# Loads laid out per group, the last two groups in halves, and a new order for every engine

## The chip, the cores and the metric

The kernel runs on one core of one Trainium2 chip. The metric is the device time of one execution in microseconds (us). A core has five engines that run in parallel, each taking its own instructions strictly in order: TensorE (PE in the profile, its weight loads PEld), VectorE (DVE), ScalarE (ACT), GpSimd (POOL) and SyncE (SP), which here only issues DMA transfers. They wait for one another by semaphores.

## The reference

Two graph layers run on 64 graphs of 128 nodes with 128 features. `adj` holds 0 or 1 in these inputs, so of the four kinds of edge in the attention layer and of the 40 relations in the second only the first occurs:

```python
e = leaky_relu(einsum('bid,bjd->bij', x * a_0, x), 0.2)     # attention scores
alpha = softmax(where(adj == 1, e, -9e15))                    # over j
y = layernorm(x + alpha @ x)
h = y @ W_loop.T
v = (h + b_loop) * sigmoid(h @ Wg_loop.T + bg_loop)
out = layernorm(y + relu((adj == 1).T @ v))
```

Values other than 0 and 1 in `adj` are answered by a slow general path at the end, which is entered only when a sum over `adj` says so. It is not entered here.

## The kernel before

The 64 graphs are 16 groups of four. Everything is done by group, in float32, as a chain of stages; a stage is one call in the code, named `stage:group` here. `products` (PE, L988) multiplies the weighed, transposed x into the scores of four graphs and adds a penalty where there is no edge (L991, from the tile `absent`). `relu` and `scores` make the leaky scores and their row maximum (DVE L877), `exp` the probabilities (ACT L775), `turn_probs` transposes them on PE (L1007), `turned_probs` copies that out of PSUM, `attend` multiplies them with x (PE L1017, tile `p_o`), `residual1` divides and adds x (DVE L883 and L888), `stats1` takes mean and variance (DVE L896), `norm1` makes the inverse root on POOL (L667 to L676), and `y_v`, `y_s`, `y_p` write the normalized y on DVE, ACT and POOL, by the table `Y_BY`. `turn_y` (PE L1033) and `turned_y` transpose y, `gates` is the product with both weight matrices (PE L1045, tile `p_hg`), `tanhs` the gate on ACT (L822), `values` gate times value on DVE (L917), `sums` the sum over neighbours (PE L1062), `residual2`, `stats2` (DVE L929, L952) and `norm2` (POOL L696 to L712) the second normalization. The table `OUT_BY` says who writes the output: POOL alone for groups 0 to 9 (L705 and L718, inside `norm2`), DVE and ACT (`finish_v`, `finish_s`) for groups 10 to 15. `store` sends it out.

Each of the five engines takes its stages in the order of one list by hand, `ORDER`. Nothing reorders them later, so an engine whose next stage has to wait keeps all that stands behind it waiting. Most tiles have two buffers, group g taking number g % 2; the PSUM tiles `p_o`, `p_e`, `p_ut`, `p_yt`, `p_hg` and `p_ag` have one.

`load_scores:g` fetches the transposed x (`x_t`) and `adj` of a group, `load_values:g` x itself; each is 256 KB on SP's queue, as 512 runs of 512 bytes (only `adj` of group 0 goes through ACT's queue). `load_weights` fetches the matrices of all three directions, two of which only the general path reads; `prepare_w`, `mix_weights` and `evac_weights` turn the loop direction's into `w_both`. The last group alone has its `sums`, `residual2`, `stats2` and `store` in halves of two graphs: their sums go to `p_ut` and `p_e`, which are free by then.

Of the kernel before, what the change touches and what calls it, by code (L numbers as in the profile page):

```python
# [33 lines left out]
OUT_BY = ["pppp"] * 10 + ["vvss"] * 5 + ["vvvs"]  # L34
# [19 lines left out]
        weigh_s:11 exp:10 tanhs:5 weigh_s:12 relu_s:11 y_s:7 exp:11 turned_y:6 mask:6 y_s:8 turned_probs_s:10
        relu_s:12 weigh_s:13 tanhs:6 exp:12 turned_y:7 weigh_s:14 y_s:9 turned_probs_s:11 relu_s:13 weigh_s:15 tanhs:7
        absent:14 turned_probs_s:12 turned_y:8 exp:13 mask:8 relu_s:14 y_s:10 tanhs:8 turned_y:9 exp:14 y_s:11 tanhs:9
        turned_probs_s:13 relu_s:15 turned_y:10 mask:10 exp:15 tanhs:10 turned_probs_s:14 turned_y:11 y_s:12
        turned_probs_s:15 tanhs:11 turned_y:12 y_s:13 tanhs:12 mask:12 turned_y:13 finish_s:10 y_s:14 tanhs:13
# [1045 lines left out]
```

## Time and profile before

| | |
|---|---|
| median of 3 runs | 114.0 us (113.84 to 115.27) |
| the profiled execution's own time | 113.89 us |
| span of its profile | 112.10 us |
| busy: PE, DVE, ACT, POOL | 99.2, 95.5, 88.5, 80.9 us |
| granted TensorE clock | 0.977 of full speed over the span, full speed until 106 us |

The span runs from the first to the last event of the core; 1.79 us of the execution's own time lie around it. Busy is the time in which at least one instruction of the engine was under way. A matmul record of the 128x128 kind lasts about 0.27 us, though the next follows after 0.11 us, so a busy PE is not a PE without gaps.

### The profile page before, as it was taken

The page shows a single profiled execution, that of the slowest core. Times are in us where ns is not written, and L with a number is a line of the kernel's source. Part 1 is how long each engine was busy: PE and PEld are TensorE (multiplying, and loading weights), DVE is VectorE, ACT ScalarE, POOL GpSimd, SP SyncE. Part 2 cuts the span into 40 slices and gives each one's busy share as a digit, 9 for nine tenths or more (in the row PEclk, how much of TensorE's full clock was granted, in tenths as well). Part 3 has the DMA queues.
Part 4 walks back from the last instruction along what each step waited for, and adds up shares of the span by engine and source line. Part 5 has one row for each costly group of instructions (what it writes and reads, how often), then busy time and mean ns, then how long its engine had stood idle before and what let it go on. Part 6 is the DMA issues. An engine that isn't in the chain of part 4 may idle for free.

```text
span 112.1 us, 2748 instructions
## 1 busy us (share of the span) xinstructions
PE 99.2 (89%) x684; PEld 88.7 (79%) x684; DVE 95.5 (85%) x376; ACT 88.5 (79%) x220; POOL 80.9 (72%) x158
## 2 busy tenths in 40 slices
PE   6997879999999999999999999999999998999000
PEld 6964767989999999998999899988899794979000
DVE  0178899799899999999998999998997999788850
ACT  4168659989999999999899989949977885896140
POOL 5004792358826799989899999999998988855560
PEclk9999999999999999999999999999999999999955
DMA  0999999999999604990423025527212030333324
GB/s 10 306 290 291 290 315 308 293 287 283 285 293 292 174 3 121 266 260 13 128 63 94 0 79 145 159 76 204 66 50 79 3 96 0 94 94 88 105 64 126
DMA packets 34771, 17.36 MB, mean 155 GB/s; under 512 B 1218, under 2 KB 34755, under 8 KB 34755
## 3 DMA queue, kind: packets, MB, share of 16 engines
q1 hardware_dynamic: 34082, 16.91, 56.6%
q10 hardware_dynamic: 672, 0.26, 0.9%
q8 instruction: 6, 0.10, 0.4%
q14 instruction: 11, 0.08, 0.2%
HBM read 12.98 MB, written 4.19 MB: 153 GB/s over the span
## 4 chain that ended last, share of the span: by engine, by line
POOL 35%; PE 27%; issue 14%; DVE 10%; ACT 5%; DMA 5%; POOLq 1%; SPq 0%; ACTq 0%; DVEq 0%
POOL rs L708 8%; POOL cent L705 7%; POOL rs L672 7%; PE p_hg L1045 6%; PE p_o L1017 5%; DMA inputs<-x_t 5%; PE p_ag L1062 3%; PE p_e L988 3%; POOL out_s L718 3%; PE p_ut L1007 3%; POOL y L687 2%; PE p_yt L1033 2%; POOL rs L696 2%; DVE res L888 2%; POOL minus L669 2%
## 5 line engine op out<-in xcount | busy, mean ns | idle before, releaser
L1045 PE MATMUL p_hg<-w_both,y_t 128*128 128x256 f32 x128 | 30.8, 384 | 0.5 <-ACT y_t L814 0.3
L1045 PEld LDWEIGHTS p_hg<-w_both,y_t 128*128 128x128 f32 x128 | 23.2, 190 | 3.8 <-ACT y_t L814 1.0
L775 ACT ACTIVATE prob<-nscore,nmax 128x128 f32<-128x128 f32 x64 | 20.3, 396 | 2.7 <-DVE nmax L877 2.6
L888 DVE SCALAR_TENSOR_TENSOR res<-p_o,rz,inputs 128x128 f32<-128x128 f32 x64 | 18.0, 344 | 1.4 <-POOL y L687 0.9
L1017 PE MATMUL p_o<-inputs,prob_t 128*128 128x129 f32 x128 | 17.2, 276 | 0.8 <-DVE prob_t L866 0.8
L1017 PEld LDWEIGHTS p_o<-inputs,prob_t 128*128 128x128 f32 x128 | 15.7, 191 | 1.7 <-DVE prob_t L866 1.0
L672 POOL TENSOR_TENSOR rs<-rs,minus_half 128x4 f32<-128x4 f32 x16 | 16.7, 1042 | 0.0
L708 POOL TENSOR_TENSOR rs<-rs,minus_half 128x4 f32<-128x4 f32 x16 | 16.3, 1020 | 0.0
L1062 PE MATMUL p_ag<-vals,mask 128*128 128x128 f32 x120 | 16.0, 276 | 0.3 <-DVE vals L917 0.3
L1062 PEld LDWEIGHTS p_ag<-vals,mask 128*128 128x128 f32 x120 | 14.9, 191 | 0.8 <-issue 0.6
L988 PE MATMUL p_e<-inputs,xat 128*128 128x128 f32 x104 | 13.9, 277 | 0.0
L656 POOL TENSOR_TENSOR xat<-inputs,a_col 128x512 f32<-128x512 f32 x6 | 6.2, 1041 | 10.6 <-DMA inputs<-x_t 7.9
L792 ACT ACTIVATE y<-res,shift,rs 128x128 f32<-128x128 f32 x26 | 11.7, 488 | 2.2 <-POOL shift L676 2.2
L822 ACT ACTIVATE th<-p_hg 128x256 f32<-128x256 f32 x32 | 11.3, 379 | 2.6 <-PE p_hg L1045 2.5
L988 PEld LDWEIGHTS p_e<-inputs,xat 128*128 128x128 f32 x104 | 12.9, 192 | 0.5 <-DVE nmax L877 0.2
L917 DVE SCALAR_TENSOR_TENSOR vals<-th,p_hg 128x256 f32<-128x256 f32 x32 | 12.1, 413 | 1.1 <-ACT th L822 1.0
L877 DVE CUSTOM_DVE_ANT_0 nscore<-p_e,rel 128x128 f32<-128x128 f32 x52 | 11.9, 285 | 0.7 <-ACT rel L767 0.7
L952 DVE BATCH_NORM_STATS2 st<-res 128x6 f32<-128x256 f32 x32 | 12.1, 420 | 0.1
L896 DVE BATCH_NORM_STATS2 st<-res 128x6 f32<-128x256 f32 x32 | 12.1, 419 | 0.0
L929 DVE SCALAR_TENSOR_TENSOR res<-p_ag,y 128x512 f32<-128x512 f32 x15 | 10.3, 684 | 1.4 <-POOL out_s L718 0.7
L1033 PE MATMUL p_yt<-ident,y 128*128 128x128 f32 x64 | 10.8, 278 | 0.5 <-ACT y L792 0.2
L718 POOL TENSOR_TENSOR out_s<-cent,rs 128x512 f32<-128x512 f32 x10 | 10.4, 1041 | 0.8
(88 smaller groups left out, 177.1 us busy)
## 6 DMA issues: line engine op xcount, KB each, us to landing
inputs<-x_t SPq DMA_DIRECT2D x16, 256.0 KB, 5.2
inputs<-x SPq DMA_DIRECT2D x16, 256.0 KB, 5.3
inputs<-adj SPq DMA_DIRECT2D x15, 256.0 KB, 5.3
out<-out_s SPq DMA_DIRECT2D x15, 256.0 KB, 2.4
inputs<-adj ACTq DMA_DIRECT2D x1, 256.0 KB, 4.5
out<-out_s SPq DMA_DIRECT2D x2, 128.0 KB, 1.9
w_rows<-w SPq DMA_DIRECT2D x1, 192.0 KB, 4.9
wg_s<-wg_t SPq DMA_DIRECT2D x1, 192.0 KB, 4.7
```

The lines of the kernel that those rows point to most:

```text
L672: nc.gpsimd.tensor_tensor(rs1[:, k, 1], rs1[:, k, 0], minus_half[:], ALU.pow).then_inc(rstd1_done, 1)
L708: nc.gpsimd.tensor_tensor(rs2[:, k, 1], rs2[:, k, 0], minus_half[:], ALU.pow).then_inc(rstd2_done, 1)
L718: nc.gpsimd.tensor_tensor(out_s[:, k], cent[:], rs2[:, k, 1, :, None].broadcast_to([P, G, P]), ALU.mult).then_inc(out_by_p, 1)
L775: nc.scalar.activation(prob[:, k, i], nscore[:, k, i], ACT.Exp, scale=-1.0, bias=nmax[:, k, i:i + 1]).then_inc(exp_done, 1)
L888: nc.vector.scalar_tensor_tensor(out=res1[:, k, i], in0=p_o[:, i // 2, i % 2, 0:P], scalar=rz[:, k, i:i + 1], in1=x_s(g)[:, i, 0:P], op0=A ...
L896: nc.vector.bn_stats(st1[:, k, half(h)].rearrange("p a c -> p (a c)"), res1[:, k, half(h)].rearrange("p a d -> p d a")).then_inc(st1_done, 1)
L917: nc.vector.scalar_tensor_tensor(out=vals[:, k, half(h)], in0=th[:, k, half(h)], scalar=1.0, in1=p_hg[:, half(h), 0], op0=ALU.add, op1=ALU ...
L988: nc.tensor.matmul(e_bank(g)[:, i], xat[:, k, i], xt(g)[:, i], start=(i == 0), stop=False, skip_group_check=True)
L1017: last = nc.tensor.matmul(p_o[:, i // 2, i % 2, 0:P + 1], prob_t[:, g % 2, i], x_s(g)[:, i], start=True, stop=True)
L1033: last = nc.tensor.transpose(p_yt[:, i], y[:, g % 4, i], ident[:])
L1045: last = nc.tensor.matmul(p_hg[:, i], y_t[:, g % 2, i], w_both[:], start=True, stop=True)
L1062: last = nc.tensor.matmul(p_sum[:, i], mask[:, s * G + i], vals[:, g % 2, i], start=True, stop=True)
```

## The change

- `x_t` and `adj` are laid out on the host so that the four graphs of a group lie side by side in a row: a group's transfer is 128 runs of 2 KB in place of 512 runs of 512 bytes. x and the output keep their runs of 512 bytes.
- `load_weights` fetches the loop direction alone; `load_others` fetches the other two later, under a semaphore of its own.
- The last two groups (`SPLIT`) run in halves from the gates on: gates, tanhs, values, sums, residual2, stats2, norm2, finish and store. The sums of group 14 go to `p_ag` and `p_o`, those of group 15 to `p_ut` and `p_e`. Their outputs are written by DVE alone (before: two graphs of group 14 and one of group 15 by ACT).
- All five lists of `ORDER` are new.

```diff
-OUT_BY = ["pppp"] * 10 + ["vvss"] * 5 + ["vvvs"]
+OUT_BY = ["pppp"] * 10 + ["vvss"] * 4 + ["vvvv"] * 2
...
     "gpsimd": """
-        ... norm2:9
-        norm2:10 norm1:14 norm1:15 norm2:11 norm2:12 norm2:13 norm2:14 norm2:15
+        ... norm2:8 norm1:14
+        norm2:9 norm2:10 norm2:11 norm1:15 norm2:12 norm2:13 norm2_h0:14 norm2_h1:14 norm2_h0:15 norm2_h1:15
...
-        load_scores:0 load_scores:1 load_values:0 load_scores:2 load_scores:3 load_scores:4 load_scores:5
-        load_values:1 load_weights:0 load_values:2 load_scores:6 load_scores:7 load_values:3 load_values:4
+        load_scores:0 load_scores:1 load_scores:2 load_scores:3 load_weights:0 load_scores:4 load_values:0
+        load_scores:5 load_scores:6 load_values:1 load_scores:7 load_values:2 load_values:3 load_values:4
...
-        last_ag = (p_ut, p_e)
+        late_ag = ((p_ag[:, 0:2], p_o[:, 0, :, 0:P]), (p_ut[:, 0:2], p_e[:, 0:2]))
...
-                sp.dma_start(xt(g), x_t_v[g]).then_inc(xt_loaded[g], 16)
+                sp.dma_start(xt(g).rearrange("p g d -> p (g d)"), x_t[g]).then_inc(xt_loaded[g], 16)
...
+            def load_others(g):
+                sp.dma_start(w_rows[:, FWD:], w[FWD:].rearrange("k f d -> f k d")).then_inc(others_loaded, 16)
+                sp.dma_start(wg_s[:, FWD:], wg_t[FWD:].rearrange("k f e -> f k e")).then_inc(others_loaded, 16)
...
+            def norm2_half(g, h):
+                k = g % 2
+                moved = [i for i in graphs_by("s", OUT_BY, g) if i // 2 == h]
+                pool.wait_ge(st2_done, 2 * g + h + 1)
+                all_out(pool, g - 2)
+                nc.gpsimd.tensor_scalar(rs2[:, k, 0, half(h)], st2[:, k, half(h), 2], 1.0 / P, EPS, ALU.mult, ALU.add)\
+                    .then_inc(var2_done, 1)
+                pool.wait_ge(var2_done, normed(g, h))
+                nc.gpsimd.tensor_tensor(rs2[:, k, 1, half(h)], rs2[:, k, 0, half(h)], minus_half[:, half(h)], ALU.pow)\
+                    .then_inc(rstd2_done, 1)
...
-            def gates(g):
+            def gates(g, hs=(0, 1)):
...
-                for h in range(2):
+                for h in hs:
                     if g >= 1:
                         pe.wait_ge(vals_done[h], g)
...
+    def rows_of_groups(a):
+        a = np.asarray(a)
+        return a.reshape(a.shape[0] // G, G, P, P).swapaxes(1, 2).reshape(a.shape[0] // G, P, W)
```

Three places of the new order follow, each as the built kernels have it. In the changed kernel norm1 stands on L702 to L711 and norm2 on L731 to L753 (its halves on L761 and L764); PE's products are L1054 and L1057, turn_probs L1073, attend L1083, turn_y L1099, gates L1111 and sums L1132.

POOL near the end, before: norm1:15 (L667 to L676), then norm2:11 (L696 to L712).

```order
L667 TENSOR_SCALAR rs<-st 128x4
L669 TENSOR_SCALAR minus<-st 128x3
L672 TENSOR_TENSOR rs<-rs,minus_half 128x4
L676 TENSOR_TENSOR shift<-minus,rs 128x3
L696 TENSOR_SCALAR rs<-st 128x4
L700 TENSOR_SCALAR minus<-st 128x2
L708 TENSOR_TENSOR rs<-rs,minus_half 128x4
L712 TENSOR_TENSOR shift<-minus,rs 128x2
```

POOL at the same place, now: norm2:11 (L731 to L747), then norm1:15.

```order
L731 TENSOR_SCALAR rs<-st 128x4
L735 TENSOR_SCALAR minus<-st 128x2
L743 TENSOR_TENSOR rs<-rs,minus_half 128x4
L747 TENSOR_TENSOR shift<-minus,rs 128x2
L702 TENSOR_SCALAR rs<-st 128x4
L704 TENSOR_SCALAR minus<-st 128x3
L707 TENSOR_TENSOR rs<-rs,minus_half 128x4
L711 TENSOR_TENSOR shift<-minus,rs 128x3
```

The last group's norm1 has changed places with norm2:11, which has to wait for stats2:11.

PE's last stages, before: gates:14, turn_y:15, sums:13, gates:15, sums:14, and sums:15 in halves.

```order
L1045 MATMUL p_hg<-w_both,y_t 128x256 x4
L1033 MATMUL p_yt<-ident,y 128x128 x4
L1062 MATMUL p_ag<-vals,mask 128x128 x4
L1045 MATMUL p_hg<-w_both,y_t 128x256 x4
L1062 MATMUL p_ag<-vals,mask 128x128 x4
L1062 MATMUL p_ut<-vals,mask 128x128 x2
L1062 MATMUL p_e<-vals,mask 128x128 x2
```

PE's last stages, now: the first half of gates:14, sums:13, the other half, turn_y:15, half of sums:14, gates:15, and three more halves of sums.

```order
L1111 MATMUL p_hg<-w_both,y_t 128x256 x2
L1132 MATMUL p_ag<-vals,mask 128x128 x4
L1111 MATMUL p_hg<-w_both,y_t 128x256 x2
L1099 MATMUL p_yt<-ident,y 128x128 x4
L1132 MATMUL p_ag<-vals,mask 128x128 x2
L1111 MATMUL p_hg<-w_both,y_t 128x256 x4
L1132 MATMUL p_o<-vals,mask 128x128 x2
L1132 MATMUL p_ut<-vals,mask 128x128 x2
L1132 MATMUL p_e<-vals,mask 128x128 x2
```

sums:13 has moved ahead of turn_y:15, and less work stands behind turn_y:15.

PE's first stages after products:0, before: products:1, turn_probs:0, attend:0, products:2, turn_probs:1, products:3.

```order
L988 MATMUL p_ag<-inputs,xat 128x128 x4
L991 MATMUL p_ag<-absent,penalties 128x512
L1007 MATMUL p_ut<-ident,prob 128x128 x4
L1017 MATMUL p_o<-inputs,prob_t 128x129 x4
L988 MATMUL p_yt<-inputs,xat 128x128 x4
L991 MATMUL p_yt<-absent,penalties 128x512
L1007 MATMUL p_ut<-ident,prob 128x128 x4
L988 MATMUL p_hg<-inputs,xat 128x128 x4
L991 MATMUL p_hg<-absent,penalties 128x512
```

The same place, now: products:1, turn_probs:0, products:2, products:3, turn_probs:1, attend:0.

```order
L1054 MATMUL p_ag<-inputs,xat 128x128 x4
L1057 MATMUL p_ag<-absent,penalties 128x512
L1073 MATMUL p_ut<-ident,prob 128x128 x4
L1054 MATMUL p_yt<-inputs,xat 128x128 x4
L1057 MATMUL p_yt<-absent,penalties 128x512
L1054 MATMUL p_hg<-inputs,xat 128x128 x4
L1057 MATMUL p_hg<-absent,penalties 128x512
L1073 MATMUL p_ut<-ident,prob 128x128 x4
L1083 MATMUL p_o<-inputs,prob_t 128x129 x4
```

The first attend has moved behind two products and a turn_probs, as x of group 0 has moved back in SP's list. ACT's list now has absent:2 and mask:0 ahead of exp:1.

## Rows read from the trace of the kernel before

**Rows 1.** The page: span, busy time by engine, and GB/s in 40 slices.
```profile
span 112.1 us, 2748 instructions
PE 99.2 (89%) x684; PEld 88.7 (79%) x684; DVE 95.5 (85%) x376; ACT 88.5 (79%) x220; POOL 80.9 (72%) x158
...
GB/s 10 306 290 291 290 315 308 293 287 283 285 293 292 174 3 121 266 260 13 128 63 94 0 79 145 159 76 204 66 50 79 3 96 0 94 94 88 105 64 126
```

**Rows 2.** The table of two windows, columns in its first line.
```profile
core 0: us, PE busy (x) PEld busy (x) DVE busy (x) ACT busy (x) POOL busy (x), PEclk, DMA share, GB/s
39.20:94.10 54.90, 54.19 (x382) 49.22 (x381) 52.01 (x197) 47.86 (x119) 51.07 (x85) 1.00 0.35 97
22.00:38.00 16.00, 16.00 (x119) 14.93 (x118) 14.93 (x67) 15.51 (x38) 10.27 (x24) 1.00 1.09 286
```

**Rows 3.** Timeline of POOL: start, us, instruction, idle time before it.
```profile
39.22 0.20 POOL L696 TENSOR_SCALAR rs<-st 128x4 f32<-128x4 f32 x1
...
42.47 0.20 POOL L696 TENSOR_SCALAR rs<-st 128x4 f32<-128x4 f32 x1
...
53.53 0.59 POOL L687 TENSOR_SCALAR y<-res,minus,rs 128x128 f32<-128x128 f32 x1
...
90.22 0.20 POOL L696 TENSOR_SCALAR rs<-st 128x4 f32<-128x4 f32 x1
...
92.08 0.20 POOL L667 TENSOR_SCALAR rs<-st 128x4 f32<-128x4 f32 x1
...
94.12 0.20 POOL L667 TENSOR_SCALAR rs<-st 128x4 f32<-128x4 f32 x1
...
95.95 0.20 POOL L676 TENSOR_TENSOR shift<-minus,rs 128x3 f32<-128x3 f32 x1
```

**Rows 4.** Timeline of the first 17 us: what waited for the loads, and exp:1.
```profile
9.17 1.04 POOL L656 TENSOR_TENSOR xat<-inputs,a_col 128x512 f32<-128x512 f32 x1 [7.15 <-DMA inputs<-x_t]
...
10.59 1.28 ACT L775 ACTIVATE prob<-nscore,nmax 128x128 f32<-128x128 f32 x4 [0.31 <-DVE nmax L877]
...
10.94 1.04 POOL L656 TENSOR_TENSOR xat<-inputs,a_col 128x512 f32<-128x512 f32 x1 [0.73 <-DMA inputs<-x_t]
...
11.79 1.06 ACT L740 ACTIVATE absent<-inputs 128x1024 bf16<-128x1024 int32 x1
...
15.39 1.06 ACT L740 ACTIVATE absent<-inputs 128x1024 bf16<-128x1024 int32 x1 [2.44 <-issue]
```

**Rows 5.** Timeline of DVE: the stages of one group, from scores:5 on.
```profile
22.54 0.29 DVE L877 CUSTOM_DVE_ANT_0 nscore<-p_e,rel 128x128 f32<-128x128 f32 x1 [0.67 <-ACT rel L767]
...
23.39 0.18 DVE L883 RECIPROCAL rz<-p_o 128x4 f32<-128x4 f32 x1
...
24.64 0.75 DVE L896 BATCH_NORM_STATS2 st<-res 128x6 f32<-128x256 f32 x2
...
25.31 0.60 DVE L907 SCALAR_TENSOR_TENSOR y<-res,st,rs 128x128 f32<-128x128 f32 x2
...
25.83 0.74 DVE L917 SCALAR_TENSOR_TENSOR vals<-th,p_hg 128x256 f32<-128x256 f32 x2
...
29.77 0.69 DVE L929 SCALAR_TENSOR_TENSOR res<-p_ag,y 128x512 f32<-128x512 f32 x1
```

**Rows 6.** Timeline of the last 14 us: PE, POOL, DVE and SP.
```profile
98.24 0.60 PE L1033 MATMUL p_yt<-ident,y 128*128 128x128 f32 x4
...
99.99 1.99 PE L1045 MATMUL p_hg<-w_both,y_t 128*128 128x256 f32 x8 [0.26 <-ACT y_t L814]
...
103.16 0.61 PE L1062 MATMUL p_e<-vals,mask 128*128 128x128 f32 x4
...
106.82 0.20 POOL L696 TENSOR_SCALAR rs<-st 128x4 f32<-128x4 f32 x1
...
108.36 0.90 DVE L944 SCALAR_TENSOR_TENSOR out_s<-res,st,rs 128x128 f32<-128x128 f32 x3 [1.20 <-POOL rs L708]
...
109.70 0.47 SPq L630 DMA_DIRECT2D out<-out_s  x1
```

More of the change, by code:

```diff
@@ L54 @@
[L54 to L58, printed above, removed]
@@ L76 @@
+        residual2:11 stats2:11 stats1:15 finish_v:10 values:13 residual2:12 finish_v:11 stats2:12 y_v:15 values_h0:14
+        residual2:13 stats2:13 values_h1:14 finish_v:12 residual2_h0:14 finish_v:13 stats2_h0:14 values_h0:15
+        residual2_h1:14 values_h1:15 stats2_h1:14 residual2_h0:15 stats2_h0:15 residual2_h1:15 stats2_h1:15
+        finish_v_h0:14 finish_v_h1:14 finish_v_h0:15 finish_v_h1:15
         """,
     "gpsimd": """
[L78 removed]
@@ L534, in groups_of @@
             by = stage[-1]
+            if stage[-3:] in ("_h0", "_h1"):
+                by = stage[-4]
+                if stage.startswith("finish_"):
+                    return [g for g in SPLIT if by in OUT_BY[g][half(int(stage[-1]))]]
+                return SPLIT
+            if stage in ("gates", "tanhs", "values", "sums", "residual2", "stats2", "norm2", "store"):
+                return [g for g in range(n_groups) if g not in SPLIT]
             if stage in PAIRED:
                 return PAIRED[stage]
-            if stage in ("load_weights", "prepare_w", "mix_weights", "evac_weights"):
+            if stage in ("load_weights", "load_others", "prepare_w", "mix_weights", "evac_weights"):
                 return [0]
@@ L547, in groups_of @@
             if stage.startswith("finish_"):
-                return [g for g in range(n_groups) if by in OUT_BY[g]]
+                return [g for g in range(n_groups) if g not in SPLIT and by in OUT_BY[g]]
             return range(n_groups)
@@ L576, in out_groups, with normed, shifts, out_made_half @@
             return sum(by in of for of in OUT_BY[:max(0, g + 1)])
+        def normed(g, h=1):
+            before = g + sum(of < g for of in SPLIT)
+            return before + (h + 1 if g in SPLIT else 1)
+        def shifts(g, h=1):
+            before = out_groups("s", g - 1) + sum("s" in OUT_BY[of][0:2] and "s" in OUT_BY[of][2:4]
+                                                  for of in SPLIT if of < g)
+            if g not in SPLIT:
+                return before + 1
+            return before + sum("s" in OUT_BY[g][half(i)] for i in range(h + 1))
+        def out_made_half(by, g, h):
+            return out_made(by, g - 1) + OUT_BY[g][:2 * h + 2].count(by)
         def graphs_by(by, table, g):
```

206 lines of the change are left out of this document (120 added, 86 removed).

## The prediction

> **What bounds the kernel now.** I read the page first [rows 1]: PE is busy for 99.2 of 112.1 us and DVE for 95.5, ACT 88.5, POOL 80.9, so nobody is a bound with room to spare and the shares alone decide nothing. Then the windows [rows 2]. From 39.2 to 94.1 us PE is busy for 54.19 of 54.90 us, DVE for 52.01, and POOL, which the page had last, for 51.07; from 22 to 38 us POOL has only 10.27 of 16 while PE has all 16 and DVE 14.93. Then POOL's own timeline [rows 3]. At 39.22 norm2:0 starts, at 94.12 norm1:15, and the pieces in between fill the stretch (the 3.8 us that are not busy are short gaps between instructions that need each other, and lie inside the pieces). A norm2 that also writes the output takes 42.47 - 39.22 = 3.25 us, a norm1 94.12 - 92.08 = 2.04, the y of one graph about 0.55, a norm2 without output 92.08 - 90.22 = 1.86. Ten, nine, five and one of these are 32.5 + 18.4 + 2.75 + 1.86 = 55.5 us, where 54.9 were measured. So POOL runs without a pause from 39.2 us until the last y can be made (its shift at 95.95), and it is what lets group 15 into the second layer. PE and DVE follow close behind it. The end hangs on a chain [rows 6]: turn_y:15 at 98.24, gates:15 at 99.99, the last sums at 103.16 to 103.77, POOL's last norm2 at 106.82 (POOL had norm2:14 before it), the last three outputs on DVE from 108.36 to 109.26, the last store issued at 109.70 and the end of the span at 112.1. From the last sum to the end that is 8.33 us.
>
> **The sum is made against the profiled execution**, 112.1 us of span and 113.89 us of its own time, 1.79 us around it. That execution lies 0.1 us under the median of 114.0. A measurement of this kernel can tell about 2%, 2.3 us, from no change.
>
> **The head: the new layout.** In the trace of before, x_t:2, the sixth transfer, lands at 9.17, x_t:3, the eighth, at 10.94, and adj:5, the thirteenth, at 15.39, where ACT had waited for it [rows 4]. That is 6.22 us for seven, 0.889 us for 256 KB, and counted back 3.84 us before the first. Nothing in the trace has runs of 2 KB. The bounds are 0.889 (no gain), and the fastest slice of the load phase, 315 GB/s [rows 1], 0.83 us; I take 0.83 and keep 0.889. A gain beyond 315 GB/s isn't excluded; its worth is small, as the next steps show. New order: adj:3 is the eighth, not the ninth, and lands at 3.84 + 8 x 0.83 = 10.5 (at 0.889: 11.0; before 11.8). absent:2 takes 1.06 us and its read-out, mask:0 as much, and only then comes exp:1 with 1.28: it ends at 10.5 + 1.2 + 1.1 + 1.3 = 14.1, where before it ended at 11.87. So turn_probs:1, the DVE copy of it (a 512-wide pass, 0.69 us as in [rows 5]) and attend:0 end at 14.2, 15.0 and 16.0. x of group 0, now at position 11.5, lands at 13.4 (14.1 at 0.889) and is in time.
>
> From there DVE sets the pace, with the prices of [rows 5]: four scores 0.85, residual1 1.25 (I use 1.3), stats 0.7, y 0.6, values 0.74, residual2 0.69. From attend:0 at 16.0: residual1:0 to 17.3, stats1:0 18.0, turned_probs:2 18.7, scores:4 19.6, residual1:1 20.9, stats1:1 21.6, y:0 22.2, scores:5 23.0, residual1:2 24.3, stats1:2 25.1. Before it ended at 25.39 with the same stages done. x of group 1 (position 16.5: 17.5, or 18.5) is needed by attend:1 for residual1:1 at 19.6, so it is in time at either pace. **The head is worth -0.3 us** with 0.83, +0.2 with 0.889. The weights of the other directions, 256 KB that go behind the early loads, are in this count. load_others is free: only the general path waits for it, and behind it on SP stand the loads of groups 10 and later.
>
> A rule of the Trainium skill speaks against the layout (DMA: Bandwidth & Descriptors, Specifications): transfers reach line rate from 512 bytes up. The runs of before have just that, so by this rule the pace stays 0.889 and the sum is 0.5 us higher. The same page (Why small descriptors are slow) gives a fixed cost of about 3 cycles for each packet beside one cycle for 32 bytes; an estimate from it is 4 x 19 cycles against 67, a pace of 0.78, and the sum would be some 0.3 us lower. No run here shows either yet.
>
> **The middle: norm2 earlier.** DVE's list now has residual2:0 and stats2:0 right behind scores:7. From 25.1 the stages ahead are y, scores, residual1, values, stats, y, residual1, stats, y, scores, residual2, stats: 9.8 us, and 0.7 more for the 7% that DVE idles here [rows 2], so norm2:0 starts at 35.6 and ends at 38.9; before it started at 39.22, and POOL idled 5.7 us between 22 and 38. norm1:5, done by 39.2 before, comes behind it at 39.0 (stats1:5 is 3.4 us of DVE further on). What POOL then has until the end of norm1:15: nine norm2 (29.3), eleven norm1 (22.4), six y (3.3) and two short norm2 (3.7), 58.7 us, less the 0.6 by which the same sum was too long before: 58.1. So norm1:15 ends at **97.1, 1.0 us later than before**, though norm2:11 now stands ahead of it with 1.86 us: the earlier start pays only half of it. The last y is then written by ACT (three passes, about 1.3 us) and turn_y:15 can't end before 98.8; by PE's work it stands 0.9 us (sums:13) further back than before. Between 98.24 and 98.24 + 0.9 = 99.1 I put its start at 98.5.
>
> **The tail: halves.** Behind turn_y:15 there were sums:13, gates:15, sums:14, sums:15, now only half of sums:14, gates:15 and three halves of 0.45 us. turn_y:15 ends at 98.9, tanh and the copy by ACT follow to 99.6, gates:15 runs 99.7 to 101.4, and the last half of the sums, which waits for a tanh behind finish_s:13, ends at 103.0, against 103.77. On DVE stats of the first half of group 14 end at 101.4, behind finish_v:13. POOL has four half norm2: from 106.82 to 108.36 it took 1.54 us for a whole one with a small extra instruction of 0.2 [rows 6], so 1.3 us each if half the width costs the same. The nearest row of less work is the small multiplication of 0.20 us [rows 3], which bounds the power from below; I take the full price, since the row is the same operation. They end at 102.8, 104.6, 105.9 and 107.2 (the second waits for its stats at 103.2). DVE adds the 0.9 us of three graphs that ACT wrote before, but in the shadow of POOL, and its last half (two graphs, 0.6 us) ends at 107.9. At the low end POOL is never waited for: DVE's stats of the last half end at 104.7, and four halves of the output of 0.6 us each end at 107.1 to 107.2. The last store no longer stands behind another (0.4 us): issued at 107.9, and 2.4 us to the end as before (109.70 to 112.1) gives 110.3, or 109.6.
>
> **The sum:** span between 109.6 and 110.3, and I take 110.0: 2.1 us less. With 1.79 around it the time is **111.8 us**, 1.9% under the median. If the cover goes (POOL late), the halves cost up to two powers more, 2 us, and the tail gives nothing.
>
> **Rivals.**
> - *The runs of 2 KB are no faster.* By the pace of [rows 4] everything in the head stands 0.5 us later: 112.3 us. For it: 290 GB/s in nearly every slice may be a limit of the memory and not of the runs.
> - *The new order opens holes elsewhere.* In 54.9 us of the middle PE has 0.7 us idle, DVE 2.9, POOL nothing but its short gaps [rows 2, 3]. An order so tight has little to win and can lose: two holes of 0.7 us on POOL, or norm2:0 no earlier than before, and the result is 113.3 us. Against it: POOL had 5.7 us of idle to give.
> - *POOL is ahead by more.* If DVE doesn't idle on its way to stats2:0 and the power on two elements is short, norm1:15 ends at 96.2 and the tail follows PE, -1.5 us: 110.3 us.
> - *Slower: norm2:11 in front of norm1:15.* On POOL norm2:11 must wait for stats2:11, which hangs on sums:11, behind attend:15 and gates:12 on PE. POOL comes to it at 97.1 - 2.04 - 1.86 = 93.2 us. Each us by which stats2:11 ends later moves norm1:15, the last y and the end by one us. From 95.3 us on the kernel is slower than before; at 96.4 it is 115.0 us. For it: before, residual2:11 was on DVE only at 92.8. Against it: its place on DVE is now ahead of stats1:15.
>
> **How the numbers follow.** Forecast 0.32 (its own range 110.9 to 112.7), no faster runs 0.18, holes 0.18, POOL ahead 0.22, norm2:11 late 0.10. Faster by over 2% means under 111.7: all of POOL ahead, a good 0.4 of the forecast, a third of the case of no faster runs, together 0.42. Slower by over 2%, above 116.3, is the far part of the last case, 0.04, and 0.54 are left. The range reaches from the case of POOL ahead with a margin, 109.6, to the upper side of the holes, 114.3; outside lie some 0.15, most of it the case of norm2:11.
>
> **What would show it.** Right: GB/s of the load phase above 315; the first norm2 of POOL at 35 to 37 us; no idle on POOL from there until norm1:15 ends at about 97; half norm2 of 1.3 us; the last sum at 103 and the end 7.3 us behind it. Wrong: a wait of POOL for stats2:11 or stats1:15 near 93, a wait of PE for y before turn_y:15, DVE idle above 3 us in the middle, or attend:0 waiting for x.

## The result, and the profile after

| kernel | median us | lowest to highest | runs | span of the profiled execution |
|---|---|---|---|---|
| before | 114.12 | 113.84 to 115.27 | 4 | 112.1 |
| after | 109.38 | 109.15 to 109.69 | 4 | 107.4 |

The ratio is 0.956, with a 95% interval of 0.951 to 0.961: 4.4% faster; by the medians it is 4.7 us. Six executions, four of layout_alone and two of after_norm1_first, ran at a lower granted clock and over 1.5% longer, and are left out of every ratio and median here. The forecast was 111.8 us with a range of 109.6 to 114.3, so the direction is right and the time lies 0.2 us below the range. The span was forecast at 110.0 and is 107.4.

The page of after, its first lines and the row of GB/s in 40 slices; they answer to [rows 1]:

```profile
span 107.4 us, 2765 instructions
PE 97.9 (91%) x677; PEld 89.4 (83%) x684; DVE 94.4 (88%) x380; ACT 87.1 (81%) x217; POOL 81.0 (75%) x158
...
GB/s 15 307 407 367 373 350 297 352 350 388 330 53 0 5 294 95 195 0 201 278 312 97 98 9 113 180 72 26 73 27 6 98 6 98 98 98 46 156 77 124
```

POOL has no less to do: it was busy for 80.9 us and is busy for 81.0, so on POOL the 4.7 us are idle time that is gone. DVE was busy for 95.5 us and PE for 99.2, now 94.4 and 97.9. The load phase runs at 350 to 407 GB/s in most slices where it ran at about 290.

The table of windows of after, columns in its first line, which answers to [rows 2]; the first two are of the load phase:

```profile
core 0: us, PE busy (x) PEld busy (x) DVE busy (x) ACT busy (x) POOL busy (x), PEclk, DMA share, GB/s
6.00:10.00 4.00, 3.55 (x24) 2.67 (x24) 3.21 (x16) 2.86 (x9) 2.08 (x2) 1.00 1.05 391
10.00:16.00 6.00, 5.95 (x43) 4.82 (x43) 5.86 (x31) 5.03 (x14) 3.12 (x3) 1.00 1.08 360
22.00:38.00 16.00, 15.95 (x117) 14.88 (x117) 15.42 (x68) 15.74 (x40) 12.55 (x26) 1.00 0.57 184
33.10:92.70 59.60, 58.70 (x429) 55.64 (x431) 56.74 (x221) 55.41 (x138) 54.49 (x95) 1.00 0.35 103
```

Between 22 and 38 us POOL does 12.55 us of work, where it did 10.27. That is the work it would otherwise have had to do at the end.

POOL's timeline of after (start, us, instruction, idle time before it), which answers to [rows 3]; L731 begins a norm2, L702 a norm1:

```profile
33.11 0.23 POOL L731 TENSOR_SCALAR rs<-st 128x4 f32<-128x4 f32 x1 [0.17 <-DVE st L1013]
...
36.72 0.20 POOL L702 TENSOR_SCALAR rs<-st 128x4 f32<-128x4 f32 x1 [0.18 <-DVE st L955]
...
38.95 0.20 POOL L731 TENSOR_SCALAR rs<-st 128x4 f32<-128x4 f32 x1 [0.40 <-DVE st L1013]
...
90.75 0.20 POOL L731 TENSOR_SCALAR rs<-st 128x4 f32<-128x4 f32 x1
...
92.66 0.20 POOL L702 TENSOR_SCALAR rs<-st 128x4 f32<-128x4 f32 x1
...
94.50 0.30 POOL L711 TENSOR_TENSOR shift<-minus,rs 128x3 f32<-128x3 f32 x1
```

norm2:0 starts at 33.11, 6.1 us earlier than before. After 38.95 POOL waits for no other engine until norm1:15 (one gap of 0.25 us, at 78, is its own), which starts at 92.66 although norm2:11 (90.75) now stands ahead of it, where it started at 94.12 without.

The head of after, timeline of POOL, ACT, PE and DVE; the first two rows answer to [rows 4], the last is stats1:2:

```profile
7.37 1.04 POOL L691 TENSOR_TENSOR xat<-inputs,a_col 128x512 f32<-128x512 f32 x1 [5.34 <-DMA inputs<-x_t]
...
9.36 1.04 ACT L795 ACTIVATE absent<-inputs 128x1024 bf16<-128x1024 int32 x1
...
12.93 1.07 PE L1083 MATMUL p_o<-inputs,prob_t 128*128 128x129 f32 x8
13.78 0.68 DVE L925 COPY prob_t<-p_ut 128x512 f32<-128x512 f32 x1
...
15.21 0.18 DVE L942 RECIPROCAL rz<-p_o 128x4 f32<-128x4 f32 x1
...
23.11 0.76 DVE L955 BATCH_NORM_STATS2 st<-res 128x6 f32<-128x256 f32 x2
```

x_t:2 is used at 7.37 instead of 9.17, absent:2 runs at 9.36 instead of 11.79, and stats1:2 ends at 23.87 instead of 25.39.

The tail of after, timeline of PE, POOL, DVE and SP, which answers to [rows 6]:

```profile
95.33 1.14 PE L1099 MATMUL p_yt<-ident,y 128*128 128x128 f32 x4
...
97.16 1.99 PE L1111 MATMUL p_hg<-w_both,y_t 128*128 128x256 f32 x8 [0.23 <-ACT y_t L871]
...
100.64 0.68 PE L1132 MATMUL p_e<-vals,mask 128*128 128x128 f32 x4 [0.23 <-DVE vals L976]
...
101.87 0.19 POOL L761 TENSOR_SCALAR rs<-st 128x2 f32<-128x2 f32 x1
102.15 0.69 POOL L764 TENSOR_TENSOR rs<-rs,minus_half 128x2 f32<-128x2 f32 x1
102.82 0.19 POOL L761 TENSOR_SCALAR rs<-st 128x2 f32<-128x2 f32 x1
103.10 0.70 POOL L764 TENSOR_TENSOR rs<-rs,minus_half 128x2 f32<-128x2 f32 x1
...
102.33 2.17 DVE L1005 SCALAR_TENSOR_TENSOR out_s<-res,st,rs 128x128 f32<-128x128 f32 x8
...
102.95 2.24 SPq L663 DMA_DIRECT2D out<-out_s  x4
```

turn_y:15 ends at 96.47, the last sums at 101.32, and from there to the end of the span it is 6.1 us, where it was 8.33. DVE writes all eight graphs in one piece of 2.17 us and waits for no power of POOL (the last one ends at 103.80, and the last two graphs, which need it, are a quarter of the piece).

### The profile page after: what moved, and what is told of

It is laid out like the page before. It is cut to its first block, busy times and chain, and to the rows that moved or that the text cites. A ratio compares the mean times of both kernels' runs of the same rounds, so it can differ in the third digit from the quotient of the medians.

```text
span 107.4 us, 2765 instructions
## 1 busy us (share of the span) xinstructions
PE 97.9 (91%) x677; PEld 89.4 (83%) x684; DVE 94.4 (88%) x380; ACT 87.1 (81%) x217; POOL 81.0 (75%) x158
## 4 chain that ended last, share of the span: by engine, by line
POOL 38%; DVE 23%; issue 18%; PE 14%; ACT 3%; POOLq 1%; DVEq 0%; ACTq 0%
POOL rs L707 9%; POOL cent L740 8%; POOL rs L743 7%; DVE nscore L936 5%; DVE res L947 5%; PE p_ag L1038 4%; PE p_hg L1111 3%; DVE rel L918 2%; POOL minus L704 2%; POOL out_s L753 2%; POOL rs L731 2%; PE p_e L1054 2%; POOL rs L702 2%; DVE out_s L1005 2%; POOL y L722 2%
## 5 line engine op out<-in xcount | busy, mean ns | idle before, releaser
L1111 PE MATMUL p_hg<-w_both,y_t 128*128 128x256 f32 x128 | 30.6, 381 | 0.9 <-ACT y_t L871 0.9
L1111 PEld LDWEIGHTS p_hg<-w_both,y_t 128*128 128x128 f32 x128 | 23.0, 190 | 3.8 <-ACT y_t L871 1.3
L1083 PE MATMUL p_o<-inputs,prob_t 128*128 128x129 f32 x128 | 17.2, 276 | 0.2 <-DVE res L947 0.2
L1083 PEld LDWEIGHTS p_o<-inputs,prob_t 128*128 128x128 f32 x128 | 15.9, 191 | 1.0 <-issue 0.7
L707 POOL TENSOR_TENSOR rs<-rs,minus_half 128x4 f32<-128x4 f32 x16 | 16.6, 1037 | 0.0
L1132 PE MATMUL p_ag<-vals,mask 128*128 128x128 f32 x116 | 15.4, 275 | 0.2
L1132 PEld LDWEIGHTS p_ag<-vals,mask 128*128 128x128 f32 x116 | 14.8, 191 | 0.4
L1054 PE MATMUL p_e<-inputs,xat 128*128 128x128 f32 x104 | 14.2, 281 | 0.2 <-DVE nmax L936 0.2
L743 POOL TENSOR_TENSOR rs<-rs,minus_half 128x4 f32<-128x4 f32 x14 | 14.3, 1021 | 0.0
L1054 PEld LDWEIGHTS p_e<-inputs,xat 128*128 128x128 f32 x104 | 13.3, 197 | 0.6 <-DVE nmax L936 0.4
L1073 PE MATMUL p_ut<-ident,prob 128*128 128x128 f32 x64 | 10.8, 280 | 0.5 <-ACT prob L830 0.4
L753 POOL TENSOR_TENSOR out_s<-cent,rs 128x512 f32<-128x512 f32 x10 | 10.4, 1041 | 0.8
L740 POOL TENSOR_TENSOR cent<-res,st 128x512 f32<-128x512 f32 x10 | 10.6, 1058 | 0.0
```

The source lines that it names most:

```text
L707: nc.gpsimd.tensor_tensor(rs1[:, k, 1], rs1[:, k, 0], minus_half[:], ALU.pow).then_inc(rstd1_done, 1)
L740: nc.gpsimd.tensor_tensor(cent[:], res2[:, k], st2[:, k, :, 1:2].broadcast_to([P, G, P]), ALU.subtract).then_inc(cent_done, 1)
L743: nc.gpsimd.tensor_tensor(rs2[:, k, 1], rs2[:, k, 0], minus_half[:], ALU.pow).then_inc(rstd2_done, 1)
L753: nc.gpsimd.tensor_tensor(out_s[:, k], cent[:], rs2[:, k, 1, :, None].broadcast_to([P, G, P]), ALU.mult).then_inc(out_by_p, 1)
L1054: nc.tensor.matmul(e_bank(g)[:, i], xat[:, k, i], xt(g)[:, i], start=(i == 0), stop=False, skip_group_check=True)
L1083: last = nc.tensor.matmul(p_o[:, i // 2, i % 2, 0:P + 1], prob_t[:, g % 2, i], x_s(g)[:, i], start=True, stop=True)
```

## The experiments

Each row has the kernel's ratio to the kernel before (measured beside it, with medians from 113.85 to 114.13) with its 95% interval, its median, and from its trace the starts of norm2:0 and norm1:15 on POOL, of turn_y:15 and of the last half of the sums on PE, and the end of the span, all in us.

| kernel | ratio | median | norm2:0 | norm1:15 | turn_y:15 | last sums | end |
|---|---|---|---|---|---|---|---|
| before | 1 | 114.0 | 39.22 | 94.12 | 98.24 | 103.16 | 112.1 |
| layout_alone | 1.006 (1.001 to 1.012) | 114.56 | 39.44 | 94.29 | 98.40 | 103.31 | 112.3 |
| before_halves | 0.999 (0.995 to 1.002) | 113.86 | 39.27 | 94.16 | 100.21 | 105.03 | 111.7 |
| before_halves_2 | 0.995 (0.991 to 0.999) | 113.48 | 39.12 | 93.95 | 98.07 | 103.26 | 111.2 |
| before_pool_load | 1.018 (1.017 to 1.020) | 115.98 | 39.21 | 96.11 | 100.22 | 105.15 | 114.1 |
| order_alone | 0.989 (0.984 to 0.994) | 112.79 | 34.47 | 93.83 | 96.51 | 101.50 | 110.9 |
| after_old_layout | 0.966 (0.958 to 0.974) | 110.41 | 34.41 | 93.77 | 96.45 | 101.75 | 108.6 |
| after_whole_groups | 0.978 (0.969 to 0.986) | 111.75 | 33.34 | 92.91 | 95.58 | 100.58 | 109.9 |
| after | 0.956 (0.951 to 0.961) | 109.38 | 33.11 | 92.66 | 95.33 | 100.64 | 107.4 |
| after_norm2_late | 0.985 (0.982 to 0.988) | 112.02 | 39.18 | 95.70 | 98.38 | 103.68 | 110.4 |
| after_pool_load | 0.979 (0.973 to 0.985) | 111.78 | 33.20 | 94.91 | 97.55 | 102.88 | 109.5 |
| after_dve_load | 0.976 (0.974 to 0.978) | 111.11 | 32.95 | 94.46 | 97.14 | 102.44 | 109.2 |
| after_norm1_first | 0.967 (0.961 to 0.973) | 110.34 | 33.00 | 90.96 | 96.15 | 101.62 | 108.5 |
| after_group9_by_act | 0.975 (0.972 to 0.978) | 111.07 | 32.77 | 94.15 | 96.59 | 102.09 | 108.9 |

### The layout, alone and taken back

layout_alone is the kernel before with the runs of 2 KB and nothing else:

```diff
-                sp.dma_start(xt(g), x_t_v[g]).then_inc(xt_loaded[g], 16)
+                sp.dma_start(xt(g).rearrange("p g d -> p (g d)"), x_t[g]).then_inc(xt_loaded[g], 16)
...
-                    sp.dma_start(adj_s(g), adj_v[g]).then_inc(adj_loaded[g], 16)
+                    sp.dma_start(adj_s(g).rearrange("p g d -> p (g d)"), adj_rows[g]).then_inc(adj_loaded[g], 16)
```

> The kernel before, with x_t and adj in runs of 2 KB and nothing else changed. The loads move at 367 to 407 GB/s in the trace after, against 290 before. Theory (the gain of the head is loads that land earlier, in an order that uses it): with the old order DVE is held at x_t:1, absent:2 and adj:5 only, some 1.0 to 1.5 us of its idle time before 17 us go, and since POOL is then bound from norm2:0 on, the end moves by about 1 us: 112.5 to 113.3. Rival A (the layout is the main part of the change): 111 or less. Rival B (the old order can't use it): 113.8 to 114.2.

Measured: 0.6% slower, and the end of the span at 112.3, so the theory's gain did not come. The transfers are about as fast as in after. The windows of layout_alone over the load phase:

```profile
6.00:10.00 4.00, 3.00 (x17) 1.77 (x15) 3.04 (x12) 3.18 (x9) 1.41 (x2) 1.00 1.06 379
10.00:16.00 6.00, 5.06 (x41) 4.78 (x42) 5.55 (x27) 4.64 (x13) 3.76 (x7) 1.00 1.11 361
```

absent:4 runs at 12.99 instead of 15.39, and still norm2:0 starts 0.2 us later. The timeline of layout_alone, POOL and DVE, shows where a loss can come from; the last row is residual1:1:

```profile
16.97 1.04 POOL L654 TENSOR_TENSOR xat<-inputs,a_col 128x512 f32<-128x512 f32 x1
...
17.16 1.26 DVE L905 SCALAR_TENSOR_TENSOR y<-res,st,rs 128x128 f32<-128x128 f32 x2
...
20.73 1.13 DVE L886 SCALAR_TENSOR_TENSOR res<-p_o,rz,inputs 128x128 f32<-128x128 f32 x4
```

In before the same two DVE passes take 0.61 us, from 17.13, and POOL runs nothing between 17.13 and 19.11, since its x_t comes later. Here POOL's pass over 512 columns is on at that time, DVE's passes take 0.65 us more, and residual1:1 starts 0.67 us later than in before (20.06). At this place the old order hangs on DVE's list and not on the transfers. That these 0.67 us are the whole of the loss at the end is not shown. The Trainium skill (SBUF — State Buffer, Who interferes with whom) says that a DVE instruction with two inputs in SBUF contends with a GpSimd instruction that reads SBUF, and calls the ports that they share an exclusive lock. If DVE's passes could start only behind POOL's, they would end at 18.01 + 0.60 = 18.6; the trace has 18.42, so it agrees with the contention, and the passes are not kept out for quite the whole of it.

after_old_layout is the same edit the other way: the kernel after with runs of 512 bytes for x_t and adj.

> The changed kernel with x_t and adj back in runs of 512 bytes; order, halves and late weights kept. Theory: the new order packs the loads close to use, so adj:3 and x of group 0 land 1 to 1.5 us later, attend:0 and all of the head follow, norm2:0 starts about 1.3 us later and POOL carries that to the end: 110.4 to 111.2. Rival A (layout is the main part): 112 or more. Rival B (the head has room): 109.3 to 109.7.

Measured: 1.0 us slower than after by the medians, 1.2 in the span. norm2:0 comes 1.3 us later, norm1:15 1.1, turn_y:15 1.1, the last sums 1.1. In the new order a later load passes through every stage to the end, in the old order it passes through none. Of the 6.1 us by which norm2:0 is earlier in after, the layout has 1.3 and the order 4.8.

### The order alone, the halves alone

order_alone has the new lists and the late weights, whole groups at the end, the outputs and the layout of before:

```diff
-OUT_BY = ["pppp"] * 10 + ["vvss"] * 4 + ["vvvv"] * 2
+OUT_BY = ["pppp"] * 10 + ["vvss"] * 5 + ["vvvs"]
...
-        ... gates_h0:14 sums:13 gates_h1:14 turn_y:15 sums_h0:14 gates_h0:15 gates_h1:15 sums_h1:14 sums_h0:15 sums_h1:15
+        ... gates:14 sums:13 turn_y:15 gates:15 sums:14 sums:15
...
-        ... norm2:13 norm2_h0:14 norm2_h1:14 norm2_h0:15 norm2_h1:15
+        ... norm2:13 norm2:14 norm2:15
```

> The new order with whole groups at the end, runs of 512 bytes; of the change only the order (with the late weights that are part of SP's list). The layout cost 1.0 us when it was taken from the changed kernel and the halves 2.4 us, so if the parts add up beside the order: 109.4 + 1.0 + 2.4 = 112.8 us (112.3 to 113.2). Rival (what bounds the end without the halves isn't the head, so the layout is hidden there): 111.7 to 112.0.

after_whole_groups is the same with the runs of 2 KB.

> The changed kernel with the end of before: groups 14 and 15 whole (only the last sums, residual and store in halves as before), two outputs of group 14 and one of group 15 by ACT again, the rest of the order as changed. Theory: the last sum comes at about 101.5 as in the changed kernel, and from there it takes 8.3 us as before instead of 6.1: 111.0 to 111.8. Rival (the halves only move work, the gain is all from norm2 and the loads being earlier): 109.2 to 110.2.

Measured against before: the order brings 1.1%, with the layout 2.2%, with the halves too 4.4%. By the medians the three steps are 1.2, 1.0 and 2.4 us. Steps taken one upon the other always add up to the whole; what tests the sum is order_alone, which was put at 112.8 us from the parts taken out of after one at a time, and took 112.79. So beside the new order the layout is worth 1.0 us with the halves and without them. What whole groups cost at the end is in the timeline of after_whole_groups, POOL and DVE:

```profile
102.41 0.20 POOL L703 TENSOR_SCALAR rs<-st 128x4 f32<-128x4 f32 x1 [1.75 <-DVE st L959]
...
104.25 0.20 POOL L703 TENSOR_SCALAR rs<-st 128x4 f32<-128x4 f32 x1
...
105.78 0.90 DVE L951 SCALAR_TENSOR_TENSOR out_s<-res,st,rs 128x128 f32<-128x128 f32 x3 [1.19 <-POOL rs L715]
```

The last sums start at 100.58, as in after (100.64). But POOL can begin norm2:14 only when all of group 14 has its stats (a wait of 1.75 us), norm2:15 has to stand behind it, and DVE waits 1.19 us for the last power. So the halves don't bring the sums forward; all of their 2.4 us lies behind the last sum.

before_halves and before_halves_2 put the halves on the kernel before, with its layout and its order up to group 13. They differ in the lists of the last two groups. The last stages of PE and ACT in the one and the other:

```diff
-PE:  gates_h0:14 sums:13 gates_h1:14 turn_y:15 sums_h0:14 gates_h0:15 gates_h1:15 sums_h1:14 sums_h0:15 sums_h1:15
+PE:  gates_h0:14 gates_h1:14 turn_y:15 sums:13 gates_h0:15 sums_h0:14 gates_h1:15 sums_h1:14 sums_h0:15 sums_h1:15
-ACT: tanhs:13 mask:14 turned_y:14 finish_s:11 tanhs_h0:14 y_s:15 tanhs_h1:14 turned_y:15 finish_s:12 tanhs_h0:15 ...
+ACT: mask:14 y_s:14 tanhs:13 turned_y:14 y_s:15 finish_s:11 tanhs_h0:14 tanhs_h1:14 turned_y:15 finish_s:12 tanhs_h0:15 ...
```

> The kernel before (its layout, its order until the last two groups, weights loaded early) with the halves at the end and its last two groups' outputs on DVE alone. Theory: the tail alone, 1.5 to 2.2 us less: 111.9 to 112.7. Rival (without the earlier POOL the halves find nothing to overlap, because turn_y:15 waits as before): 113.4 to 114.2.

> The kernel before with halves at the end, in a second list of the last two groups: the mask of groups 14 and 15 is made before y:14 and y:15 is written by ACT before the tanh of group 14, both of which stood in the way in the run before_halves (PE waited 0.83 us for the transposed y of group 14). Theory (in the old order the tail can gain only what POOL's late norm1:15 leaves; turn_y:15 starts at 98.2 as before, and from there half of the sums, the gates and three halves follow): last sum at 103.8 as before, end 6.1 us behind it: 111.6 to 112.6. Rival (the halves are worth nothing without the new order): 113.5 to 114.2.

The first gave nothing, because its list put the last mask ahead of the copy that PE waited for (0.83 us) and sums:13 (0.9) ahead of turn_y:15. The timeline of before_halves, ACT and PE:

```profile
95.81 1.05 ACT L812 ACTIVATE mask<-inputs 128x1024 f32<-128x1024 int32 x1
...
97.48 1.13 PE L1116 MATMUL p_hg<-w_both,y_t 128*128 128x256 f32 x4 [0.83 <-ACT y_t L876]
```

The end behind the last sum was short there too (6.7 us from its start, against 8.9 in before), but the sum itself started 1.9 us later. With the better list the sums are where they were, and 0.5 us is gained by the ratio (0.9 in the span of the profiled execution, the fastest of twelve), not 2.4. The median of 113.48 misses the theory and stands at the edge of the rival. The timeline of before_halves_2, POOL and DVE:

```profile
101.27 0.22 POOL L736 TENSOR_SCALAR rs<-st 128x4 f32<-128x4 f32 x1 [1.20 <-DVE st L1018]
...
105.34 0.41 DVE L998 SCALAR_TENSOR_TENSOR res<-p_e,y 128x256 f32<-128x256 f32 x1
```

From the last values at 102.69 on DVE waits for nobody, but behind them stands work that after has done ahead of them: the second residual2 of group 14 and two outputs of group 13 (0.60 us, at 103.69). So its last residual2 starts at 105.34, 2.1 us behind the last sum, where in after it is 0.9. Group 13 is late here from its sums on: sums:13 starts at 98.50 (93.58 in after), POOL waits 1.20 us for stats2:13, and norm2:13 starts at 101.27 (96.75 in after). Which part of the new order brings it forward, no run separates.

### Is POOL the bound, before and after?

after_pool_load and before_pool_load add two passes of 1.04 us, whose result nobody reads, to POOL ahead of norm2:3. The values of the kernel don't change.

```diff
             def norm2(g):
                 k = g % 2
+                if g == 3:
+                    for i in range(2):
+                        nc.gpsimd.tensor_tensor(extra[:, i], xt(0).rearrange("p g d -> p (g d)"),
+                                                a_col[:].broadcast_to([P, W]), ALU.mult).then_inc(extra_done, 1)
```

> The changed kernel with two more instructions on POOL, products of 128x512 into a tile that nobody reads, ahead of norm2:3 (1.04 us each, 2.1 us in all). Theory (POOL is saturated from norm2:0 to norm1:15 and carries the delay to the end): 1.7 to 2.2 us more, 111.1 to 111.6. Rival (PE and DVE are just as close and POOL has slack): under 1 us more, 109.5 to 110.3.

> The kernel before with the same two instructions of 1.04 us on POOL ahead of norm2:3. Theory (POOL is saturated from 39.2 us on here too): 1.7 to 2.3 us more, 115.7 to 116.4. Rival (before, the end hangs on PE or on the tail's own chain): under 1 us more.

Measured: the 2.08 us come out at the end whole in both. In before norm1:15 starts 1.99 us later and the end is 2.0 later; in after it is 2.25 and 2.1 (2.4 by the medians, slightly above the theory). So POOL had no slack from norm2:3 on in either order, as the sum of its pieces said ahead of the result.

after_norm2_late undoes the early norm2 alone:

```diff
-        y_p:4 norm2:0 norm1:5 norm2:1 y_p:5 norm1:6
+        y_p:4 norm1:5 y_p:5 norm2:0 norm2:1 norm1:6
```

> The changed kernel with norm2:0 and norm2:1 behind norm1:5 and y_p:5 on POOL, as before. norm2:0 would then start at about 39 us in place of 33.1. Theory (it is the early start of norm2 that feeds POOL: in the trace after POOL idles only 2.4 us between 22 and 34, and it would idle 3.3 us more): 2 to 3.3 us more, 111.4 to 112.7. Rival (the gain came from the head): 109.3 to 110.2.

Its POOL timeline:

```profile
36.80 0.20 POOL L705 TENSOR_SCALAR rs<-st 128x4 f32<-128x4 f32 x1 [3.78 <-DVE st L958]
...
39.18 0.19 POOL L734 TENSOR_SCALAR rs<-st 128x4 f32<-128x4 f32 x1
...
95.70 0.20 POOL L705 TENSOR_SCALAR rs<-st 128x4 f32<-128x4 f32 x1
```

POOL waits 3.78 us for stats1:5, in which norm2:0 had been done in after. norm2:0 starts at the time of before (39.18), norm1:15 3.0 us later than in after, the end 3.0 (2.6 by the medians). With that one step taken back, after stands 1.5% in front of before, where it stood 4.4%.

after_dve_load adds three passes with two inputs in SBUF to DVE, ahead of values:3:

```diff
             def values(g, hs=(0, 1)):
                 k = g % 2
+                if g == 3:
+                    for i in range(3):
+                        nc.vector.tensor_tensor(extra[:, i], xt(0).rearrange("p g d -> p (g d)"),
+                                                xt(0).rearrange("p g d -> p (g d)"), ALU.mult).then_inc(extra_done, 1)
```

> The changed kernel with three more instructions on DVE ahead of values:3, products of 128x512 into a tile that nobody reads (about 0.69 us each as other passes of that width, some 2.1 us in all), at nearly the time at which after_pool_load had its 2.1 us on POOL. Theory (POOL is the bound and DVE close behind it, idle for 1.9 us between 38 and 86 us): part of it is taken up, 0.8 to 1.8 us more, 110.2 to 111.2. Rival A (DVE bounds as much as POOL): 2.1 us or more, 111.4 to 112. Rival B (DVE has room): under 0.5 us.

Its timeline, DVE and POOL:

```profile
43.83 1.88 DVE L976 TENSOR_TENSOR extra<-inputs 128x512 f32<-128x512 f32 x3
...
47.55 1.39 DVE L968 SCALAR_TENSOR_TENSOR y<-res,st,rs 128x128 f32<-128x128 f32 x2
...
44.64 0.52 POOL L733 TENSOR_SCALAR rs<-st 128x4 f32<-128x4 f32 x1
45.13 1.49 POOL L742 TENSOR_TENSOR cent<-res,st 128x512 f32<-128x512 f32 x1
...
49.70 0.20 POOL L704 TENSOR_SCALAR rs<-st 128x4 f32<-128x4 f32 x1 [0.91 <-DVE st L957]
```

1.88 us more of DVE are 1.8 us more at norm1:15 and at the end. That is not pure slack of DVE: the passes hold up POOL itself (0.52 us where it takes 0.20 in after, 1.49 where it takes 1.05), then POOL waits 0.91 us for stats1:7. At this place POOL and DVE are both on the path. How much of the loss is the wait and how much the collision was not separated. No run added work to PE, which is busy for 58.70 of the 59.60 us between norm2:0 and norm1:15, so how much room PE had is open.

### Where POOL stops being the bound

after_norm1_first brings norm1:15 ahead of norm2:11 again, on POOL alone:

```diff
-        norm2:9 norm2:10 norm2:11 norm1:15 norm2:12
+        norm2:9 norm2:10 norm1:15 norm2:11 norm2:12
```

> The changed kernel with norm1:15 ahead of norm2:11 on POOL. In the trace after POOL has no idle time from 80 us to 98.5 and norm1:15 runs from 92.66 to 94.78; it would run from 90.8 if stats1:15 is there (it is done on DVE at 91.15). Theory (POOL's norm1:15 sets y:15, but PE has its own work until 95.3): turn_y:15 starts only 0 to 0.3 us earlier, and finish_v:11 and finish_s:11 come 2 us later, ahead of halves of group 14: 109.3 to 110.3. Rival (POOL alone bounds the end): 1.5 us less, 107.6 to 108.4.

Measured: 1.0 us slower than after by the medians, 1.1 in the span. norm1:15 does start earlier, at 90.96 instead of 92.66, and nobody can use it. The timeline, POOL, DVE, ACT and PE:

```profile
90.96 0.22 POOL L705 TENSOR_SCALAR rs<-st 128x4 f32<-128x4 f32 x1 [0.60 <-DVE st L958]
...
94.44 0.64 DVE L1008 SCALAR_TENSOR_TENSOR out_s<-res,st,rs 128x128 f32<-128x128 f32 x2 [1.79 <-POOL rs L746]
...
94.71 0.88 ACT L862 ACTIVATE out_s<-res,shift,rs 128x128 f32<-128x128 f32 x2 [2.45 <-POOL shift L750]
...
95.68 0.33 DVE L969 SCALAR_TENSOR_TENSOR y<-res,st,rs 128x128 f32<-128x128 f32 x1
...
96.15 1.24 PE L1102 MATMUL p_yt<-ident,y 128*128 128x128 f32 x4 [0.95 <-DVE y L969]
```

DVE's list has the output of group 11 ahead of y:15, and that output now waits 1.79 us for the later norm2:11; behind it stand y:15 and, on PE, turn_y:15 with a wait of 0.95. ACT's list has the same: its outputs of group 11 wait 2.45 us, and its three graphs of y:15 come behind them. The median of 110.34 is the upper edge of the theory's 109.3 to 110.3, but its reason failed: it had turn_y:15 up to 0.3 us earlier, and it is 0.8 later (96.15), since it priced the swap on POOL's list and not the instructions that are queued behind the wait on DVE's and ACT's.

after_group9_by_act takes the output of group 9 from POOL (one pass over 512 columns to subtract, one to scale) and gives it to ACT, behind mask:12:

```diff
-OUT_BY = ["pppp"] * 10 + ["vvss"] * 4 + ["vvvv"] * 2
+OUT_BY = ["pppp"] * 9 + ["ssss"] + ["vvss"] * 4 + ["vvvv"] * 2
...
-        tanhs:12 mask:12 mask:14
+        tanhs:12 mask:12 finish_s:9 mask:14
```

> The changed kernel with the output of group 9 written by ACT instead of POOL, which takes 1.4 us from POOL (a norm2 with output 3.25 us, one without 1.86) and puts four passes of 0.4 us on ACT at about 88 us. Theory (POOL bounds, so 1.4 us less of it are worth something, but PE has its own work until turn_y:15 and DVE its own): 0 to 0.8 us less, 108.6 to 109.4. Rival A (POOL alone): 108.0. Rival B (ACT is in the way of the mask and tanh:13): 109.6 to 110.5.

Measured: 1.7 us slower than after, though POOL has less work, and above all three ranges. The timeline, ACT, DVE, POOL and PE:

```profile
89.00 1.64 ACT L862 ACTIVATE out_s<-res,shift,rs 128x128 f32<-128x128 f32 x4
...
90.73 0.69 DVE L991 SCALAR_TENSOR_TENSOR res<-p_ag,y 128x512 f32<-128x512 f32 x1 [2.21 <-ACT out_s L862]
...
92.31 0.20 POOL L734 TENSOR_SCALAR rs<-st 128x4 f32<-128x4 f32 x1 [3.35 <-DVE st L1016]
...
94.15 0.20 POOL L705 TENSOR_SCALAR rs<-st 128x4 f32<-128x4 f32 x1
```

residual2:11 writes the buffer that the output of group 9 reads. ACT reads it until 90.64, DVE waits 2.21 us, stats2:11 ends at 92.2, and POOL, which is ready for norm2:11 at 89.0, waits 3.35 us. norm1:15 is 1.5 us later than in after, the end 1.5. This is the case of the prediction in which norm2:11 in front of norm1:15 decides. It didn't come in after, but the margin is small: there stats2:11 starts at 89.74 and takes 0.76 us, and POOL comes to it at 90.75, 0.25 us later. So stats2:11 ends 1.7 us later here, and 1.5 us, all but the margin, reach norm1:15: the price of one us for one. Whether an earlier place for the output on ACT would gain was not tried.

## Why the prediction was right and wrong

**The bound and the direction: right.** POOL without a pause from the first norm2 to norm1:15, and the gain from its idle time between 22 and 38 us. From the start of norm2:0 to the end of norm1:15 the sum had 97.1 - 35.6 = 61.5 us; after has 94.80 - 33.11 = 61.69. The loads added to POOL came out whole, so it was on the path and not only a full engine (at one place DVE was on it as well, in after_dve_load). That the sum of this stretch met the trace within 0.2 us is in part luck: the stages came out 0.6 us shorter than charged, and gaps of 0.18, 0.40 and 0.25 us that the sum did not have came in.

**The step that failed** is the start of norm2:0, put at 35.6 and measured at 33.11: the mechanism held, and the terms ahead of it, the head and the 9.8 + 0.7 us of the middle, were 1.2 and 1.3 us too long. The tail's terms were off both ways and nearly cancel.

**The 2.6 us that the span lies below 110.0** are three differences: turn_y:15 ends at 96.47 and not at 98.9 (-2.4), from there to the end of the last sums it is 4.85 us and not 4.1 (+0.75), and from there to the end 6.1 and not 7.0 (-0.9). The +0.75 is that gates:15 takes 1.99 us where 1.7 stood, and the last sums end 2.17 us behind it where 1.6 stood; it hid as much of the error ahead of it.

1. *The head, "the fastest slice of the load phase, 315 GB/s".* This took a slice of a phase with runs of 512 bytes as the bound for runs of 2 KB. A group of 256 KB takes 262144 / 391 GB/s = 0.67 us between 6 and 10 us and 0.73 between 10 and 16, not 0.83. absent:2 ran at 9.36, where the load alone was put at 10.5. The text said that more "isn't excluded; its worth is small": in the new order the layout was worth 1.0 to 1.2 us, not 0.5. Both sides of the rule that was weighed there failed: the Trainium skill (DMA: Bandwidth & Descriptors, Specifications) has line rate from 512 bytes up, where 290 GB/s rose to 391, and the estimate from its 3 cycles for a packet (Why small descriptors are slow) gave a pace of 0.78, where 0.67 to 0.73 were measured.
2. *The head, "turn_probs:1, the DVE copy of it and attend:0".* attend:0 needs the copy of turn_probs:0 and not that of turn_probs:1, which stands ahead of it only in PE's list. PE runs attend:0 at 12.93, before DVE copies turn_probs:1 at 13.78. attend:0 ended at 14.0 and not at 16.0. DVE, with the scores of group 3 ahead of residual1:0, came to its result only at 15.21, so 0.8 us of these 2.0 were gained there. Another 0.4 came on the way to stats1:2, which took 8.66 us and not 9.1 and ended at 23.87 and not 25.1.
3. *The middle, "9.8 us, and 0.7 more for the 7% that DVE idles here".* From the end of stats1:2 to norm2:0 it took 33.11 - 23.87 = 9.24 us. The 0.7 didn't come, and the 9.8 were too long as well: the prices listed for these stages make 9.6, and most of them are durations, where instructions of one engine overlap. What follows a y starts 0.51 us behind it where 0.6 was charged three times, and what follows a values 0.66 where it was 0.74. Steps 1 to 3 are the 2.5 us by which norm2:0 started early (33.11 and not 35.6), and they are still 2.3 at the end of norm1:15. They were the bigger part of the case "POOL is ahead by more", which had 0.22; that case put the time at 110.3 us and was 0.9 us too high as well.
4. *The tail, "I take the full price".* The power over two elements takes 0.70 us and over four 1.03, and a half norm2 follows another in 0.95, not 1.3. In the last outputs DVE never waited for POOL, so the low end of that part was the right one: stats of the last half to the first of the last outputs without a wait, eight passes in 2.17 us, where four times 0.6 stood.
5. *The rivals.* "No faster runs" fell at once. "Holes" didn't open: POOL's waits after norm2:0 are 0.18 and 0.40 us. "norm2:11 in front" is a real mechanism, with its price as worked out, shown in after_group9_by_act; in after it missed by 0.25 us. The other signs of a failure stayed away too: no wait of PE for y before turn_y:15, and DVE idle for 59.60 - 56.74 = 2.86 us in the middle.

**The range** began at 109.6, a margin below the case of POOL ahead, while the steps were given their late values: the bound of the pace, an idle share, and the full power. Head, middle and tail came out 1.2, 1.3 and 0.9 us early, all to the same side, and only the +0.75 between turn_y:15 and the last sums kept the miss at 0.2 us.

## What to carry to other kernels

Where one engine is saturated for half of the span, look for idle time of it ahead of that stretch, and move work there: here norm2:0 and norm2:1, moved by one or two places in one list, brought 2.6 us, because here such an engine passed the time on to the end nearly us for us. A part tested alone on the old order says little about its worth in the new one: the layout was worth nothing (slightly less) there and 1.0 us here, the halves 0.5 us and 2.4. Add up an engine's stages by the distance from start to start, and give terms that can only err to one side their middle and not their cautious end.
